# Seventeen more unread bf16 products on TensorE between the folded weights, the head weights and the first heads, and the early ones moved to the fourth score bank

## What is computed

```
# attention (x: b, s, d)
q_in = (x @ Wq.T + bq);  Q3 = conv1d(q_in, convq_w, 3 taps);  Q = [q_in, Q3] @ qproj.T
k_in = (x @ Wk.T + bk);  K3 = conv1d(k_in, convk_w, 3 taps);  K = [k_in, K3] @ kproj.T
tau   = sigmoid(tau2 (gelu(depthwise_conv(x, tau1_w))))
delta = sigmoid(del2 (gelu(depthwise_conv(x, del1_w))))
scores = (Q K^T / sqrt(8)) * tau + delta;  out = softmax(scores) V @ out_w.T
x = layernorm(x + out)
# cross-attention: log-gates from [x, ctx, ctx], decay matrix, C = qk * D, normalised, @ v
x = layernorm(x + xattn(x, ctx))
# feed-forward: blocks of 32 rounded to the FP6 grid, times scale, @ weight.T + bias
x = layernorm(x + ffn(x))
```

## Time and profile before

| what | value |
|---|---|
| median of 3 runs | 213.35 us (212.99 to 213.43) |
| profiled execution, its own time | 213.28 us |
| its span | 211.3 us |
| PE busy | 193.3 us (91%), 2103 matmul records |
| DVE busy | 159.6 us (76%) |
| ACT busy | 140.8 us (67%) |
| POOL busy | 102.4 us (48%) |
| mean granted clock of TensorE | 0.966 of full |

### The profile page before, as it was taken

The page is one execution under the profiler, slowest core; times in us unless marked ns, Lnnn a source line. Parts: engine busy times, 40 slices in busy tenths (PEclk is TensorE's granted clock), DMA queues, the critical chain, the costliest instruction groups (busy, mean ns, idle before and its releaser), DMA issues. The chain is left out here.

```text
span 211.3 us, 6086 instructions
## 1 busy us (share of the span) xinstructions
PE 193.3 (91%) x2103; PEld 122.0 (58%) x2103; DVE 159.6 (76%) x432; ACT 140.8 (67%) x427; POOL 102.4 (48%) x218
## 2 busy tenths in 40 slices
PE   7979999699999989999999999999897997889772
PEld 3768444246567754665676656775675764665321
DVE  2599659988989834579955999689563878789970
ACT  0352322364947989665868778687979989888643
POOL 3599076764999732616528434224152063425321
PEclk9965599999999999999999999999999999999999
DMA  6660000050000032003000021020300303000000
GB/s 163 168 162 28 0 5 2 12 149 3 2 3 0 3 116 81 33 5 100 0 5 3 2 99 28 11 94 29 100 3 3 103 27 101 28 0 28 28 25 25
DMA packets 12137, 9.38 MB, mean 44 GB/s; under 512 B 2796, under 2 KB 10828, under 8 KB 12108
## 3 DMA queue, kind: packets, MB, share of 16 engines
q1 hardware_dynamic: 11116, 8.96, 14.4%
q10 hardware_dynamic: 992, 0.04, 0.3%
HBM read 7.73 MB, written 1.27 MB: 43 GB/s over the span
## 5 line engine op out<-in xcount | busy, mean ns | idle before, releaser
L1129 DVE TENSOR_REDUCE nm<-score 128x8 f32<-128x1024 f32 x32 | 38.8, 1218 | 6.9 <-PE score L662 6.8
L520 ACT ACTIVATE prob<-score 128x1024 f32<-128x1024 f32 x32 | 32.5, 1020 | 11.1 <-PE score L674 11.0
L662 PE MATMUL score<-km,qf 32*128 32x512 f32 x128 | 33.9, 637 | 1.2 <-DVE nm L1129 0.3
L668 PE MATMUL score<-qm,kf 32*128 32x512 f32 x128 | 33.8, 636 | 0.0
L388 POOL CAST nmx<-nm 128x16 bf16<-128x16 f32 x16 | 5.5, 341 | 31.2 <-issue 26.2
L674 PEld LDWEIGHTS score<-nmT,sel 32*128 32x128 bf16 x256 | 10.1, 93 | 16.2 <-issue 16.2
L359 POOL TENSOR_SCALAR u<-xTp,dw 128x512 f32<-128x512 f32 x16 | 13.7, 868 | 10.3 <-PE score L740 5.4
L883 PE MATMUL bankPV<-prob,vw 128*32 128x128 f32 x512 | 17.2, 275 | 0.0
L583 ACT ACTIVATE dec<-dec,g 128x128 f32<-128x128 f32 x56 | 17.1, 393 | 0.0
L656 PE MATMUL bankP<-xTp,wT 128*128 128x512 f32 x36 | 16.8, 602 | 0.0
L422 POOL TENSOR_TENSOR hsl<-hs,rows 128x256 f32<-128x256 f32 (+1 forms) x9 | 6.0, 672 | 20.4 <-ACT hs L599 20.4
(11 more groups left out here) (264 smaller groups left out, 491.1 us busy)
## 6 DMA issues: line engine op xcount, KB each, us to landing
dec<-gates_out SPq DMA_DIRECT2D x7, 512.0 KB, 3.7
xt<-in_x_dram SPq DMA_DIRECT2D x4, 256.0 KB, 4.0
cin<-in_ctx_dram SPq DMA_DIRECT2D x4, 256.0 KB, 3.8
out_dram<-abT SPq DMA_DIRECT2D x7, 128.0 KB, 1.8
th<-taus_out SPq DMA_DIRECT2D x3, 256.0 KB, 3.4
xTr<-in_L_attn_convk_w_dram SPq DMA_DIRECT2D x1, 192.0 KB, 3.1
xTr<-in_L_attn_convq_w_dram SPq DMA_DIRECT2D x1, 192.0 KB, 3.7
taus_out<-th SPq DMA_DIRECT2D x3, 64.0 KB
```

The source lines that it names most:

```text
L520: nc.scalar.activation(prob[:, i % 2, k:k + 2, :].rearrange("p k s -> p (k s)"), sc[:, 512 * k:512 * (k + 2)], ACT.Exp, scale=SQ_SCALE).th ...
L662: ins = mm(sc[:, 512 * k:512 * (k + 1)], qf[r, n, :], km[r, n % (2 * CB)].rearrange("p j s -> p (j s)"), start=True, stop=True)
L668: mm(sc[:, 512 * k:512 * (k + 1)], kf[r, n, :], qm[r, n % (2 * CB)].rearrange("p j s -> p (j s)"), start=True, stop=False)
L1129: nc.vector.tensor_reduce(nm[:, i % 3, J * k:J * (k + 2)], sc[:, 512 * k:512 * (k + 2)].rearrange("p (h s) -> p h s", s=S), AX_X, ALU.max, ...
```

## The change

Seventeen `light` products are put among the steps of the head: one ahead of `hw.0`, four ahead of `mT.1`, four ahead of `wT.0`, two ahead of `tx.2`, one ahead of `wT.1`, two ahead of `cT.0`, and one each ahead of `del.0`, `tau.0` and `K.0`. All `light` products, the old twelve too, write score bank 3 (`sc[:, 1536:2048]`) in place of bank PV; that bank is first used by `tx.3`, which stands behind `K.0` and `Q.0`. In the tail three `fill` products are added: one between `hst.6` and `hT.6`, two between `hst.8` and `hT.8`; a `fill.2 fill.5` is written as `fill.7`. The other engines' orders stay as they are.

```diff
 PE_ORDER = """
-    light.8 tx.0 light.1 ab.0 light.3 mT.0 tx.1 hw.0 mT.1 wT.0 tx.2 wT.1 cT.0 del.0 tau.0 K.0 Q.0 gw.0 tx.3 K.1 cg.0 aa.0 fill.2 tau.1 fill.2 cT.1 fill.1
+    light.8 tx.0 light.1 ab.0 light.3 mT.0 tx.1 light.1 hw.0 light.4 mT.1 light.4 wT.0 light.2 tx.2 light.1 wT.1 light.2 cT.0 light.1 del.0 light.1
+    tau.0 light.1 K.0 Q.0 gw.0 tx.3 K.1 cg.0 aa.0 fill.2 tau.1 fill.2 cT.1 fill.1 aa.1 nmT.0 Q.1 v1.2 nmT.1 fill.5 v1.3 edT.0 V.0 ow.0 fill.1 v2.2 V.1
...
-                        mm(pvb[:], fil[:], fil[:].unsqueeze(1).to_broadcast([P, NH, S]), start=True, stop=True)
+                        mm(sc[:, 1536:2048], fil[:], fil[:].unsqueeze(1).to_broadcast([P, NH, S]), start=True, stop=True)
```

More of the change, by code:

```diff
@@ L55 @@
 PE_ORDER = """
-    light.8 tx.0 light.1 ab.0 light.3 mT.0 tx.1 hw.0 mT.1 wT.0 tx.2 wT.1 cT.0 del.0 tau.0 K.0 Q.0 gw.0 tx.3 K.1 cg.0 aa.0 fill.2 tau.1 fill.2 cT.1 fill.1
-    aa.1 nmT.0 Q.1 v1.2 nmT.1 fill.5 v1.3 edT.0 V.0 ow.0 fill.1 v2.2 V.1 rc.0 fill.2 v2.3 del.1 pv.0 nmT.2 K.2 v1.4 edT.1 pv.1 V.2 v2.4 pT.0 nmT.3 cm.0
-    v1.5 aT.0 nmT.4 cm.1 y1.0 v2.5 yT.0 pv.2 del.2 pv.3 gF.0 v1.6 MT.0 tau.2 pT.1 del.3 nmT.5 aT.1 tau.3 y1.1 Q.2 v2.6 Q.3 qk.0 edT.2 pv.4 edT.3 cT.2
-    hst.0 nmT.6 v1.7 cT.3 hT.0 gF.1 cm.2 v2.7 K.3 v1.8 nmT.7 pv.5 V.3 MT.1 v1.9 yT.1 pT.2 V.4 v2.8 aT.2 cm.3 dT.0 y1.2 qk.1 pv.6 ffn.0 v2.9 nmT.8 hst.1
@@ L60 @@
[L60 to L63, removed]
@@ L64 @@
-    ld.8 hT.7 dT.5 fill.2 ffn.5 fill.5 hst.8 hT.8 dT.6 fill.2 ffn.6 fill.8 dT.7 fill.2 ffn.7 fill.9 dT.8 fill.2 ffn.8
+    light.8 tx.0 light.1 ab.0 light.3 mT.0 tx.1 light.1 hw.0 light.4 mT.1 light.4 wT.0 light.2 tx.2 light.1 wT.1 light.2 cT.0 light.1 del.0 light.1
+    tau.0 light.1 K.0 Q.0 gw.0 tx.3 K.1 cg.0 aa.0 fill.2 tau.1 fill.2 cT.1 fill.1 aa.1 nmT.0 Q.1 v1.2 nmT.1 fill.5 v1.3 edT.0 V.0 ow.0 fill.1 v2.2 V.1
+    rc.0 fill.2 v2.3 del.1 pv.0 nmT.2 K.2 v1.4 edT.1 pv.1 V.2 v2.4 pT.0 nmT.3 cm.0 v1.5 aT.0 nmT.4 cm.1 y1.0 v2.5 yT.0 pv.2 del.2 pv.3 gF.0 v1.6 MT.0
@@ new lines @@
+    tau.2 pT.1 del.3 nmT.5 aT.1 tau.3 y1.1 Q.2 v2.6 Q.3 qk.0 edT.2 pv.4 edT.3 cT.2 hst.0 nmT.6 v1.7 cT.3 hT.0 gF.1 cm.2 v2.7 K.3 v1.8 nmT.7 pv.5 V.3
+    MT.1 v1.9 yT.1 pT.2 V.4 v2.8 aT.2 cm.3 dT.0 y1.2 qk.1 pv.6 ffn.0 v2.9 nmT.8 hst.1 cm.4 yT.2 v1.10 hT.1 pv.7 nmT.9 v2.10 pT.3 gF.2 v1.11 aT.3 MT.2
+    V.5 nmT.10 y1.3 v2.11 yT.3 pv.8 v1.12 V.6 pv.9 qk.2 nmT.11 cm.5 pT.4 v2.12 hst.2 gF.3 V.7 hT.2 aT.4 dT.1 v1.13 ffn.1 nmT.12 pv.10 v2.13 y1.4 V.8
+    MT.3 pv.11 v1.14 pT.5 nmT.13 cm.6 v2.14 aT.5 gF.4 v1.15 y1.5 MT.4 cm.7 qk.3 nmT.14 pv.12 yT.4 v2.15 hst.3 dT.2 cm.8 pv.13 hT.3 yT.5 bb.14 nmT.15
@@ L65 @@
+    pT.6 gF.5 ffn.2 aT.6 qk.4 y1.6 pv.14 yT.6 hst.4 bb.15 pT.7 MT.5 hT.4 aT.7 gF.6 y1.7 pv.15 dT.3 qk.5 pT.8 MT.6 ffn.3 yT.7 fill.7 gF.7 aT.8 hst.5
+    qk.6 hT.5 ld.7 dT.4 y1.8 MT.7 qk.7 ffn.4 yT.8 fill.2 hst.6 fill.1 hT.6 fill.2 gF.8 hst.7 qk.8 fill.2 MT.8 ld.8 hT.7 dT.5 fill.2 ffn.5 fill.5 hst.8
+    fill.2 hT.8 dT.6 fill.2 ffn.6 fill.8 dT.7 fill.2 ffn.7 fill.9 dT.8 fill.2 ffn.8
 """
```

## The result

| | before | changed |
|---|---|---|
| median | 213.23 us (212.89 to 214.16, 13 runs) | 212.05 us (211.03 to 212.82, 13 runs) |
| ratio | 1 | 0.9933, 95% interval 0.9917 to 0.9948 |
| profiled execution | 213.28 us, span 211.3 | 212.82 us, span 210.8 |

The change makes the kernel faster: by 0.67% by the ratio of the runs (1.4 us), by 1.2 us between the medians. 209.8 was forecast, 3.5 us less, and the range began at 208.9 and ended at 211.9. The direction held, the size was two and a half to three times too large. The runs of the changed kernel also spread over 1.8 us, and the profiled execution is the slowest of the 13; a later profile of the same kernel, taken at 212.15 us (the last experiment), is nearer to the median.

What follows compares the result with a forecast made beforehand. PE at half clock was taken to bound the head at 24.57 to 28.78 us, DVE before and after. `kf.0` gains 3.6 us, less 0.1 for `aa.0`: 213.3 - 3.5 = 209.8 us, range 208.9 to 211.9.

Steps and rivals of the forecast that it cites:

- the ceiling: Head: DVE's idle wait for `K.0` ahead of `kf.0`, 4.21 us, is the most a faster PE can give back.
- the half-clock stretch: Head, 12.6 to 26.2 us: PE runs 13.6 us at 1.2 GHz; worth 3.5 us.
- The full 6.8 us: Head: 13.6 us times 0.5 all comes back, counting PE alone; 206.5 us, chance 0.02.
- The price of an unread product: Head: 512 bf16 columns cost 0.215 us at 2.4 GHz, 0.42 at 1.2; seventeen cost 3.7 or 7.2 us.
- the walk along PE: Head, `hw.0` to `K.0`, clock holding: `K.0` starts at 21.95, readable at 24.75, 4.0 us earlier.
- DVE beside POOL: Head: POOL's taps beside `tapT.2` slow DVE by 0 to 0.75 us, taken as 0.6; `kf.0` at 25.2.
- The walk from `kf.0` to `qs.0`: Head, behind `K.0`: DVE's list from `kf.0` to the end of `qs.0` stays at 6.5 us.
- I assume that the clock holds: Head: with the added products PE stays at the high clock level, 1.00 from 12 to 28 us; chance 0.72.
- Rival 2: Head: clock holds for part only, or POOL and DVE slow each other further; gain 1 to 2.9 us, 210.4 to 212.3, chance 0.12.
- I carry the 3.5 us to the end: From `aa.0` to the end: orders untouched, waits relative to work, so the head's 3.5 us gain stays whole.
- rival 4: Later thin stretches: head gains 3.5 us, a new clock fall loses 2 to 3.5; 211.8 to 213.3, chance 0.04.
- The tail fills and the bank: Tail: three fills go into PE's waits, costing nothing or 0.1 us at `hT.8`; score bank 3 costs nothing.

Runs made afterwards that it cites:

- the last experiment: The whole change run once more, on the chip of two other runs, against the kernel before: 212.05 us against 213.47, ratio 0.9936.
- the thick tail: Four more fills, two ahead of `y1.8`, two ahead of `qk.7`: on the whole change 209.76 us, on the kernel before 212.86, each against 213.34.

## Why the prediction was wrong

**What bounds the kernel, and the ceiling.** Right in the main: the half-clock stretch was on the path through DVE's hole ahead of `kf.0`, and DVE's own work ends close behind what PE can give, so little more than half of the 6.8 us comes back. Which of the two is last depends on the case. With seventeen products it is PE in every profile, by 0.23 us where the clock held; with nine it is DVE (25.33). The full 6.8 us of the Trainium skill's rule ("TensorE: Matmul & The Clock Gate", Terms), which counts PE alone, never came near; the best kernels gained 3.6 us.

**The price of an unread product, of the walk along PE, of DVE beside POOL.** Right in size where the clock held, and the 25.10 against 25.2 owes something to luck. PE reached `K.0` at 22.33 and not at 21.95; it was late already at `hw.0`, by 0.5 us. Of `tapT.2`'s two operations one was caught (1.06), the other not (0.74), 0.3 us and not the 0.6 I took, so DVE was done at 24.87. The two misses cancel. The walk from `kf.0` to `qs.0` stayed as it was.

**"I assume that the clock holds."** This failed, and it is the smaller part. In the profiled execution the clock fell even earlier, at 11.2, and came back at 14.6. Rival 2 has it in a word, "for part only", but an earlier fall that ends after 3.4 us is in none of the rivals. Price, by the profiles of the same head: `kf.0` at 25.84 in place of 25.10, 0.7 us; 1.0 us in the execution near the median (26.11), 1.5 us in the worst (26.62).

**"From `aa.0` on the orders are untouched and every wait is relative to work, so I carry the 3.5 us to the end."** This is the step that failed most. The waits are relative; the clock's changes are not. In the tail a stretch that had held once did not hold this time, and 2.5 of 2.9 us went there, 1.5 of 2.6 in the execution near the median. Head and tail together leave 0.5 us in the one profile and 1.1 in the other, and the medians say 1.2. I had the place as rival 4, with its price (2 to 3.5 us), and gave it 0.04; the measured 212.05 also lies in rival 2's 210.4 to 212.3, but only with the loss of both places. The reason I gave, that before the change no such fall is there, was one profile. The earlier trace rows showed that the clock can hold on such a stretch, not that it does in every execution. The kernel before can fall there too, as the profile with only the three fills shows. Four fills at that very place give 209.76 us, the forecast's 209.8. What decides in a given execution whether the clock falls there stays open.

**What one profile could tell.** The Trainium skill, "TensorE: Matmul & The Clock Gate", section "What's actually happening", says of the first rise of the clock, as a kernel warms up, that its point varies by 500 ns either way. The traces show the like of a later fall, and more of it: with the products of the head unchanged the fall stood at 12.6, 13.5, 12.8 and 11.0 us in four profiles (before, and the kernels with the tail fills, the thick tail and the other bank). Had I weighed it, the fall in the head and that in the tail would both have been likely cases, and the range would have reached to 213.

**The tail fills and the bank.** Priced at nothing, and they cost nothing that shows (1.0011 and 0.9995, each to 0.0016).

## What to carry to other kernels

Where a change rests on TensorE's clock, its gain can differ from execution to execution (in one kernel here by 3.9 us): read the times and the mean clock of many runs, and take every stretch with holes or thin products as a place where the clock may fall, also far behind the edit. Look for the thinnest such place on the path, and fill its waits first; here four products in waits of 0.5 and 0.4 us decided about 1.9 us by the ratios. And put unread work only as far as the next bound asks for: nine products did here what seventeen did at their best, and kept `kf.0` at 25.33 even where the clock fell, since DVE's own work ends there.

## What the runs showed of the hardware

A mean granted clock beside each run's time sorted the runs of one kernel roughly: 0.999 went with 209.87 us and 0.968 with 213.79, in one kernel on one chip. It also counts stretches that cost nothing. With the thick tail 0.994 went with 209.70 us and 1.00 with 209.72; in the profile of the first the clock fell only behind PE's last product. The first eight unread products took 3.60 us in the profile of before and 3.49 in that of the change, about 0.42 us from start to start, and the clock column said 1.00 for both; the column doesn't show the lower level at the kernel's start, the distances do. PE's busy share alone doesn't tell where the clock falls: it fell at 11.2 us with PE busy for 2.00 of 2 us, and held from 180 to 182 with 1.21 of 2 in the profile with nine products. And the clock can come back early: at 14.6, after four unread products, `mT.1` and some more, where in the profile of before it took until `K.0` at 26.2.
